# A causal mask added by VectorE in a PSUM bank in place of a matmul per score tile

## The chip, the core and the metric

The kernel runs on one core of a Trainium2 chip. The metric is the device time of one execution in microseconds. A core has TensorE (matmuls, called PE in the profile), VectorE (DVE), ScalarE (ACT), GpSimd (POOL) and SyncE (SP, here only DMAs), each with its own instruction stream. They meet only through semaphores that the kernel sets and waits on by hand.

## What is computed

One transformer layer on an input of 4 batches, 1024 tokens and 256 features. A layer norm feeds a latent attention with 16 heads and a linear layer with binarised weights, and both are added to the input. Cut to what matters:

```python
q = jnp.concatenate([queries_c, queries_r], axis=-1)      # 128 + 64 wide, 16 heads
k = jnp.concatenate([keys_c, keys_r], axis=-1)
scores = jnp.einsum('bhqd,bhkd->bhqk', q, k) * scale
causal = jnp.triu(jnp.ones((s, s), dtype=bool), k=1)
scores = jnp.where(causal[None, None], jnp.float32(-1000000000.0), scores)
probs = jax.nn.softmax(scores, axis=-1)
ctx = jnp.einsum('bhqk,bhkd->bhqd', probs, values)
...
x = x + attention(layernorm(x)) + linear(layernorm(x))
```

Only the 128 x 128 block on the diagonal of a tile of 128 queries needs a mask: keys to its right are never computed into the softmax, and keys to its left are all allowed.

## The kernel before

**Steps, blocks, items.** A step is one pair of heads of one batch: 8 pairs by 4 batches are 32 steps. A step has four blocks n = 0 to 3. A block joins a long and a short tile of 128 queries (7 and 0, 6 and 1, 5 and 2, 4 and 3), for both heads, which gives four score items x = 0 to 3 in the order long, short, long, short. An item is therefore as wide as its keys: 1024 and 128 in block 0, 896 and 256 in block 1, 768 and 384 in block 2, 640 and 512 in block 3. The code counts blocks through the whole run with g.

**The way of an item.** PE writes the scores, with their sign turned, into a slot of `ring`, a PSUM ring of only two slots of 1024 columns that items share with the projections for the next step (`ROPE_K`, `QUERY_X`, `QUERY_Y`, three a step). Each chunk of up to 512 keys takes three matmuls in a split precision (lines 1334 to 1336). VectorE reads the slot, subtracts a column, writes `probs` and takes the minimum along the row (`minimum`, line 1069). That frees the slot. ScalarE takes the exponential (`exponent`, 883). PE transposes the probabilities in groups of up to two key tiles for two heads, four transposes a group, into one of two `turn` banks (`turn_group`, 1359). ScalarE copies the high part of a group out (`turned_high`, 892), VectorE subtracts it for the low part (`turned_low`, 1079). Five groups make a block. PE then multiplies by the latent values (`weigh_group`, 1377 and 1378, into `u_ps`) and by the output weights (`output`, 1397 and 1398, into `o_ps`), with copies by ScalarE (897, 906) and VectorE (`u_low`, 1085), and VectorE adds the result to `acc` (`accumulate`, 1115, twice, the second waiting for the first).

**What sets the order.** Every engine's order is written by hand in a `sequence(g)` of its own, in order and without skipping. PE's transposes of block g - 1 lie between the scores of block g. Before `turn_group` writes a bank it waits until `turned_low` has read the group two before; before a group of a tile begins it waits for the exponentials of both heads.

**The mask.** `mask(g, x)` on PE waits for the ring slot (`slot_left`: until the entry two before has been read) and multiplies a bfloat16 identity by a bfloat16 tile `mask_bf`, which holds 1e30 above the diagonal and 0 elsewhere. The product begins the accumulation in the diagonal block, and the last chunk of the scores adds to it. `turn_group(g, i, (g', x), ...)` puts the masks that it is given ahead of its last transpose, sometimes two at once:

```python
                        if (t, h) == (tiles - 1, 1):
                            for block_g, x in masked:
                                mask(block_g, x)
```

So it is the mask that waits for the slot, and the scores that follow need no wait of their own for it.

Of the kernel before, what the change touches and what calls it, by code (L numbers as in the profile page):

```python
# [30 lines left out]
ALU = mybir.AluOpType  # L31
# [3 lines left out]
P = 128  # L35
# [60 lines left out]
def is_block(g):  # L96
    return 0 <= g < STEPS * BLOCKS
# [382 lines left out]
def layer(nc, T, x, wp_dram, wv_dram, out):  # L480


    with ExitStack() as ctx:
# [3 lines left out]
        def sem(name):  # L487
            return ctx.enter_context(nc.semaphore(name))

        ident, ident_bf, mask_bf = T["ident"], T["ident_bf"], T["mask_bf"]  # L490
# [54 lines left out]
        min_ready = sem("min_ready")  # L545
# [9 lines left out]
        def slot_of(entry):  # L555

            return ITEM[entry] % 2
# [457 lines left out]
        def _(dve):  # L1015
# [210 lines left out]
        def _(pe):  # L1226
# [84 lines left out]
            def mask(g, x):  # L1311

                if not is_block(g):
                    return
                qt, entry = LONG_SHORT[g % BLOCKS][x % 2], ("score", g, x)
                slot_left(entry)
                pe.matmul(ring[slot_of(entry)][:, KEY_COLUMN[qt] + qt * P:KEY_COLUMN[qt] + (qt + 1) * P], ident_bf[:, :], mask_bf[:, :],  # L1317
                          start=True, stop=False, skip_group_check=True)

            def scores(g, x, c):  # L1320

                if not is_block(g):
                    return
                h, w = divmod(x, 2)
                qt, slot, entry = LONG_SHORT[g % BLOCKS][w], g // BLOCKS % 2, ("score", g, x)
                queries = slice(qt * P, (qt + 1) * P)
                qh, ql = q_hi[slot][h][:, queries], q_lo[slot][h][:, queries]
                kh, kl = k_hi[slot][h], k_lo[slot][h]

                first_key, width = KEY_CHUNKS[qt][c]  # L1330
# [9 lines left out]
            def turn_group(g, i, *masked):  # L1340
# [12 lines left out]
                for t in range(tiles):  # L1353
                    for h in range(2):
                        kt = first_kt + t
                        if (t, h) == (tiles - 1, 1):
                            for block_g, x in masked:
                                mask(block_g, x)
                        mm = pe.transpose(turn[r % 2][:, (2 * t + h) * P:(2 * t + h + 1) * P],  # L1359
                                          probs_of(g, w, h)[:, kt * P:(kt + 1) * P], ident[:, :])  # L1360
# [52 lines left out]
            def sequence(g):  # L1413
# [3 lines left out]
                if n == 0:  # L1417
# [3 lines left out]
                    turn_group(g - 1, 1, (g, 0))  # L1421
# [5 lines left out]
                    turn_group(g - 1, 2, (g, 1))  # L1427
# [4 lines left out]
                    turn_group(g - 1, 3, (g, 2))  # L1432
# [9 lines left out]
                    turn_group(g, 0, (g, 3))  # L1442
                    weigh_group(g - 1, 3)
                    scores(g, 3, 0)
                    turn_group(g, 1, (g + 1, 0))
                elif n == 1:
# [4 lines left out]
                    turn_group(g - 1, 2, (g, 1))  # L1451
# [4 lines left out]
                    turn_group(g - 1, 3, (g, 2))  # L1456
# [4 lines left out]
                    turn_group(g - 1, 4, (g, 3))  # L1461
# [4 lines left out]
                    turn_group(g, 0, (g + 1, 0))  # L1466
                elif n == 2:
                    scores(g, 0, 0)
                    scores(g, 0, 1)
                    turn_group(g - 1, 1, (g, 1))  # L1470
                    weigh_group(g - 2, 4)
                    scores(g, 1, 0)
                    turn_group(g - 1, 2, (g, 2))
# [5 lines left out]
                    turn_group(g - 1, 3, (g, 3))  # L1479
# [10 lines left out]
                    turn_group(g, 0, (g + 1, 0), (g + 1, 1))  # L1490
                    output(g - 2, 1)
                else:
# [8 lines left out]
                    turn_group(g - 1, 2, (g, 2))  # L1501
# [9 lines left out]
                    turn_group(g - 1, 4, (g, 3))  # L1511
# [44 lines left out]
```

## Time and profile before

| | |
|---|---|
| median of 3 runs | 1517.84 us (1513.96 to 1517.99) |
| the profiled execution | 1516.44 us, of which 1514.4 us are the span |
| PE busy | 1435.9 us (95%) |
| ScalarE busy | 1219.0 us (80%) |
| VectorE busy | 1160.3 us (77%) |
| GpSimd busy | 946.8 us (63%) |
| mean granted TensorE clock | 0.987 |

The span runs from the first to the last instruction. Busy time is summed over a span whose first 156 us prepare weights, so that a share over the whole understates what an engine does in the steps. Steps that carry no work for the next batch take just under 40 us each. In each of the first three batches the last three steps also prepare the next batch and take longer.

### The profile page before, as it was taken

How to read it: one execution, taken by the hardware profiler on the slowest of the kernel's cores; microseconds unless marked ns; L12 is line 12 of the kernel's file. 1: busy time of each engine (PE TensorE's matmuls, PEld its weight loads, DVE VectorE, ACT ScalarE, POOL GpSimd, SP SyncE). 2: the span in 40 equal slices, each digit the busy share in tenths (PEclk: the TensorE clock that was granted, in tenths of full speed). 3: DMA queues.
4: the chain of work that ended last, by engine and by line, in shares of the span. 5: the costliest groups of instructions: out<-in, count | busy, mean ns of one | idle time of the engine just before them, and what ended most of it. 6: DMA issues, size and time to landing. Idle time of an engine off the chain costs nothing.

```text
span 1514.4 us, 27903 instructions
## 1 busy us (share of the span) xinstructions
PE 1435.9 (95%) x9878; PEld 1300.0 (86%) x9878; DVE 1160.3 (77%) x2768; ACT 1219.0 (80%) x2568; POOL 946.8 (63%) x476
## 2 busy tenths in 40 slices
PE   1976999999999999999999999999999999999998
PEld 1855899989889999989889899989889999999987
DVE  2444688888677888888767888888767788888887
ACT  0532888899868888899878888899878888888886
POOL 3010777776767677766867577776866577777750
PEclk9996999999999999999999999999999999999998
DMA  9445232222032432222023432211123422111110
GB/s 209 160 160 124 60 88 60 60 60 60 22 88 74 108 88 60 61 60 57 19 79 89 109 88 60 60 47 44 44 73 95 109 60 59 48 47 50 53 29 29
DMA packets 46819, 111.62 MB, mean 74 GB/s; under 512 B 13600, under 2 KB 22816, under 8 KB 46688
## 3 DMA queue, kind: packets, MB, share of 16 engines
q1 hardware_dynamic: 36912, 103.31, 24.9%
q10 hardware_dynamic: 8720, 3.70, 1.1%
q0 software_dynamic: 1056, 2.89, 0.7%
q8 instruction: 79, 1.29, 0.4%
q14 instruction: 52, 0.43, 0.1%
HBM read 50.10 MB, written 13.63 MB: 42 GB/s over the span
## 4 chain that ended last, share of the span: by engine, by line
PE 80%; ACT 6%; DVE 4%; SPq 1%; POOL 1%; issue 1%; DMA 1%; DVEq 0%; POOLq 0%; ACTq 0%
PE turn L1359 15%; PE ring L1304 10%; PE u_ps L1377 8%; PE u_ps L1378 8%; PE ring L1336 8%; PE ring L1334 8%; PE ring L1335 8%; PE o_ps L1397 4%; PE o_ps L1398 4%; ACT probs L883 2%; PE ring L1317 2%; PE ring L1266 2%; PE ring L1272 1%; DVE probs L1069 1%; ACT probs_hi L892 1%; DVE probs_lo L1079 1%
## 5 line engine op out<-in xcount | busy, mean ns | idle before, releaser
L1069 DVE TENSOR_SCALAR_CACHE_REDUCE probs<-ring,c_t 128x1024 f32<-128x1024 f32 (+7 forms) x512 | 413.7, 809 | 105.7 <-PE ring L1336 103.5
L1079 DVE TENSOR_TENSOR probs_lo<-turn,probs_hi 128x512 fp32r<-128x512 f32 (+1 forms) x640 | 400.9, 630 | 70.3 <-ACT probs_hi L892 65.8
L892 ACT ACTIVATE probs_hi<-turn 128x512 fp32r<-128x512 f32 (+1 forms) x640 | 351.0, 550 | 110.2 <-PE turn L1359 105.2
L883 ACT ACTIVATE probs<-probs,row_min 128x1024 f32<-128x1024 f32 (+7 forms) x512 | 394.4, 771 | 10.8 <-DVE probs L1069 8.3
L1359 PE MATMUL turn<-ident,probs 128*128 128x128 f32 x2304 | 385.8, 275 | 7.6 <-ACT probs L883 5.2
L1359 PEld LDWEIGHTS turn<-ident,probs 128*128 128x128 f32 x2304 | 286.4, 140 | 33.9 <-ACT probs L883 11.2
L1377 PE MATMUL u_ps<-probs_hi,kv_nat 128*128 128x256 f32 x1152 | 314.6, 302 | 0.3 <-DVE probs_lo L1079 0.3
L1378 PE MATMUL u_ps<-probs_lo,kv_nat 128*128 128x256 f32 x1152 | 289.9, 281 | 0.0
L1334 PE MATMUL ring<-k_hi,q_hi 128*128 128x512 f32 (+2 forms) x768 | 280.0, 365 | 0.0
L1336 PE MATMUL ring<-k_hi,q_lo 128*128 128x512 f32 (+2 forms) x768 | 264.3, 344 | 0.0
L1335 PE MATMUL ring<-k_lo,q_hi 128*128 128x512 f32 (+2 forms) x768 | 262.9, 342 | 0.0
L1115 DVE SCALAR_TENSOR_TENSOR acc<-o_ps,row_inv,acc 128x256 f32<-128x256 f32 x480 | 229.9, 479 | 36.2 <-PE o_ps L1398 31.4
L1377 PEld LDWEIGHTS u_ps<-probs_hi,kv_nat 128*128 128x128 f32 x1152 | 218.9, 190 | 1.3 <-DVE probs_lo L1079 0.5
L1378 PEld LDWEIGHTS u_ps<-probs_lo,kv_nat 128*128 128x128 f32 x1152 | 218.5, 190 | 0.0
L608 POOL TENSOR_TENSOR k_rope<-k_rope,cos 128x1024 f32<-128x1024 f32 x31 | 74.4, 2401 | 194.9 <-DMA swapped<-k_rope 194.8
L615 POOL TENSOR_TENSOR k_lo<-k_rope,k_hi 64x1024 fp32r<-64x1024 f32 x62 | 148.2, 2390 | 58.0 <-ACT k_hi L861 55.5
L1336 PEld LDWEIGHTS ring<-k_hi,q_lo 128*128 128x128 f32 x768 | 145.0, 189 | 13.6
L608 POOL TENSOR_TENSOR q_x<-q_x,cos 64x1024 f32<-64x1024 f32 x31 | 74.4, 2399 | 131.1 <-DMA swapped<-q_x 131.1
L1334 PEld LDWEIGHTS ring<-k_hi,q_hi 128*128 128x128 f32 x768 | 147.0, 191 | 7.2
L1335 PEld LDWEIGHTS ring<-k_lo,q_hi 128*128 128x128 f32 x768 | 145.7, 190 | 7.4
L608 POOL TENSOR_TENSOR swapped<-swapped,sin 128x1024 f32<-128x1024 f32 x62 | 148.7, 2399 | 4.9
L1397 PE MATMUL o_ps<-wv,u_hi 128*128 128x256 f32 x512 | 145.2, 305 | 4.2 <-DVE acc L1115 2.3
(176 smaller groups left out, 2631.5 us busy)
## 6 DMA issues: line engine op xcount, KB each, us to landing
wp<-wp_scratch SPq DMA_DIRECT2D x32, 640.0 KB, 4.2
wv<-wv_scratch SPq DMA_DIRECT2D x32, 512.0 KB, 3.3
swapped<-k_rope SPq DMA_DIRECT2D x128, 128.0 KB, 2.3
swapped<-q_y SPq DMA_DIRECT2D x64, 128.0 KB, 2.3
swapped<-q_x SPq DMA_DIRECT2D x64, 128.0 KB, 2.3
wp_scratch<-wp_parts SPq DMA_DIRECT2D x8, 640.0 KB, 3.4
wv_scratch<-wv_parts SPq DMA_DIRECT2D x8, 512.0 KB, 4.3
k_hi<-qb_kv_hi SPq DMA_DIRECT2D x16, 256.0 KB, 3.8
```

The source lines that it names most:

```text
L608: engine.tensor_tensor(to, a, b, op).then_inc(rope_step, 1)
L883: act.activation(p, p, ACT.Exp, scale=-1.0, bias=row_min[:, r:r + 1], accum_out=row_sum[:, g % 4, w, h:h + 1]).then_inc(exp_ready, 1)
L892: act.activation(probs_hi[:, r % 4, 0:width], turn[r % 2][:, 0:width], ACT.Identity).then_inc(turned_hi, 1)
L1069: dve.tensor_scalar(probs_of(g, w, h), ring[slot_of(entry)][:, KEY_COLUMN[qt]:KEY_COLUMN[qt] + keys], c_t[b % 2][:, qt, ds(pair * 2 + h, 1 ...
L1079: dve.tensor_tensor(probs_lo[:, r % 4, 0:width], turn[r % 2][:, 0:width], probs_hi[:, r % 4, 0:width].bitcast(F32), ALU.subtract).then_inc ...
L1115: dve.scalar_tensor_tensor(out=acc[:, qt, :], in0=o_ps[:, h, :], scalar=inv, in1=start[:, qt, :], op0=ALU.mult, op1=ALU.add).then_inc((acc ...
L1334: pe.matmul(to, qh, kh[:, keys], start=not masked, stop=False, skip_group_check=masked)
L1335: pe.matmul(to, qh, kl[:, keys], start=False, stop=False, skip_group_check=masked)
L1336: mm = pe.matmul(to, ql, kh[:, keys], start=False, stop=True, skip_group_check=masked)
L1359: mm = pe.transpose(turn[r % 2][:, (2 * t + h) * P:(2 * t + h + 1) * P], probs_of(g, w, h)[:, kt * P:(kt + 1) * P], ident[:, :])
L1377: pe.matmul(u_ps[:, 0:2 * P], kv_nat[:, kt, :], probs_hi[:, r % 4, cols], start=(kt == 0), stop=False)
L1378: mm = pe.matmul(u_ps[:, 0:2 * P], kv_nat[:, kt, :], probs_lo[:, r % 4, cols], start=False, stop=(kt == qt))
```

## The change

The mask matmuls go, 16 a step and 512 in all, with the function that made them. The scores' first chunk waits for the ring slot itself, and all chunks start a fresh accumulation. VectorE adds the same mask tile to the diagonal block of the slot, in PSUM and in place, and waits on a semaphore of its own, `mask_added`, before it takes the minimum. The weights, the ring, the order of everything else and the other engines are as before.

```diff
@@ minimum, VectorE
                 dve.wait_ge(ring_full, ITEM[entry] + 1)
+                diagonal = ring[slot_of(entry)][:, KEY_COLUMN[qt] + qt * P:KEY_COLUMN[qt] + keys]
+                dve.tensor_tensor(diagonal, diagonal, mask[:, :], ALU.add).then_inc(mask_added, 1)
+                dve.wait_ge(mask_added, g * SCORE_ITEMS + x + 1)
                 dve.tensor_scalar(probs_of(g, w, h), ring[slot_of(entry)][:, KEY_COLUMN[qt]:KEY_COLUMN[qt] + keys],
@@ scores, PE
-                masked = c == len(KEY_CHUNKS[qt]) - 1
-                pe.matmul(to, qh, kh[:, keys], start=not masked, stop=False, skip_group_check=masked)
-                pe.matmul(to, qh, kl[:, keys], start=False, stop=False, skip_group_check=masked)
-                mm = pe.matmul(to, ql, kh[:, keys], start=False, stop=True, skip_group_check=masked)
-                if masked:
+                if c == 0:
+                    slot_left(entry)
+                pe.matmul(to, qh, kh[:, keys], start=True, stop=False)
+                pe.matmul(to, qh, kl[:, keys], start=False, stop=False)
+                mm = pe.matmul(to, ql, kh[:, keys], start=False, stop=True)
+                if c == len(KEY_CHUNKS[qt]) - 1:
                     mm.then_inc(ring_full, 1)
@@ turn_group, PE
-                        if (t, h) == (tiles - 1, 1):
-                            for block_g, x in masked:
-                                mask(block_g, x)
@@ sequence, PE (15 calls lose their masks)
-                    turn_group(g - 1, 3, (g, 2))
+                    turn_group(g - 1, 3)
```

On PE, in block 0 of a step in the middle of the run, item 2's mask stood inside the group of transposes ahead of item 2's scores. The rows are one instruction each (or a run of equal ones), with the tile written, the tiles read and what it waits for. Before:

```order
 L1359 MATMUL turn<-ident,probs 128x128 [waits turned_ready,exp_ready]
 L1359 MATMUL turn<-ident,probs 128x128 x2
 L1317 MATMUL ring<-mask_bf,ident_bf 128x128 [waits min_ready]
 L1359 MATMUL turn<-ident,probs 128x128
 L1334 MATMUL ring<-k_hi,q_hi 128x512 [waits k_lo_ready,hi_step,rope_step]
```

The same place after the change:

```order
 L1349 MATMUL turn<-ident,probs 128x128 [waits turned_ready,exp_ready]
 L1349 MATMUL turn<-ident,probs 128x128 x3
 L1329 MATMUL ring<-k_hi,q_hi 128x512 [waits k_lo_ready,min_ready,hi_step,rope_step]
 L1330 MATMUL ring<-k_lo,q_hi 128x512
 L1331 MATMUL ring<-k_hi,q_lo 128x512
```

The wait for `min_ready`, which frees the slot, moved behind the last transpose, to the first matmul of the scores.

On VectorE, in blocks 2 and 3 of a step, each minimum (`probs,row_min<-ring,c_t`) stood alone. Before:

```order
 L1069 TENSOR_SCALAR probs,row_min<-ring,c_t 128x640 [waits ring_full]
 L1085 TENSOR_TENSOR u_pair<-u_ps,u_hi 64x256 [waits u_hi_ready]
 L1079 TENSOR_TENSOR probs_lo<-turn,probs_hi 128x512 [waits turned_hi]
 L1069 TENSOR_SCALAR probs,row_min<-ring,c_t 128x512 [waits ring_full]
 L1115 SCALAR_TENSOR_TENSOR acc<-o_ps,row_inv,acc 128x256 [waits o_full,inv_ready]
 L1079 TENSOR_TENSOR probs_lo<-turn,probs_hi 128x512 [waits turned_hi]
```

The same place, at the start of block 3, after the change:

```order
 L1070 TENSOR_TENSOR ring<-ring,mask_bf 128x128 [waits ring_full]
 L1072 TENSOR_SCALAR probs,row_min<-ring,c_t 128x640 [waits mask_added]
 L1088 TENSOR_TENSOR u_pair<-u_ps,u_hi 64x256 [waits u_hi_ready]
 L1082 TENSOR_TENSOR probs_lo<-turn,probs_hi 128x512 [waits turned_hi]
 L1070 TENSOR_TENSOR ring<-ring,mask_bf 128x128 [waits ring_full]
 L1072 TENSOR_SCALAR probs,row_min<-ring,c_t 128x512 [waits mask_added]
 L1118 SCALAR_TENSOR_TENSOR acc<-o_ps,row_inv,acc 128x256 [waits o_full,inv_ready]
 L1082 TENSOR_TENSOR probs_lo<-turn,probs_hi 128x512 [waits turned_hi]
```

Each minimum now has the addition directly ahead of it, and the wait for the scores moved to the addition. The minimum waits for the addition.

## Rows read from the trace of the kernel before

**Rows 1.** The page, busy time of each engine, share of the span, instructions

```profile
PE 1435.9 (95%) x9878; PEld 1300.0 (86%) x9878; DVE 1160.3 (77%) x2768; ACT 1219.0 (80%) x2568; POOL 946.8 (63%) x476
```

**Rows 2.** The page, the chain that ended last, by engine and by line

```profile
PE 80%; ACT 6%; DVE 4%; SPq 1%; POOL 1%; issue 1%; DMA 1%; DVEq 0%; POOLq 0%; ACTq 0%
PE turn L1359 15%; PE ring L1304 10%; PE u_ps L1377 8%; PE u_ps L1378 8%; PE ring L1336 8%; PE ring L1334 8%; PE ring L1335 8%; PE o_ps L1397 4%; PE o_ps L1398 4%; ACT probs L883 2%; PE ring L1317 2%; PE ring L1266 2%; PE ring L1272 1%; DVE probs L1069 1%; ACT probs_hi L892 1%; DVE probs_lo L1079 1%
```

**Rows 3.** Windows: one plain step, then two that also prepare a batch

```profile
core 0: us, PE busy (x) PEld busy (x) DVE busy (x) ACT busy (x) POOL busy (x), PEclk, DMA share, GB/s
...
540.42:580.30 39.88, 39.88 (x290) 36.95 (x289) 33.75 (x81) 35.48 (x76) 28.85 (x13) 1.00 0.29 84
...
400.30:447.00 46.70, 45.18 (x275) 38.01 (x275) 29.70 (x68) 33.29 (x65) 32.51 (x14) 1.00 0.22 60
447.00:500.10 53.10, 52.19 (x384) 48.45 (x383) 41.12 (x98) 43.23 (x93) 29.43 (x14) 1.00 0.36 90
```

**Rows 4.** Groups by line and shape on VectorE: count, busy us, mean ns

```profile
L1079 DVE TENSOR_TENSOR probs_lo<-turn,probs_hi 128x512 fp32r<-128x512 f32 x512 | 347.6, 683 | 69.8 <-ACT probs_hi L892 65.3
...
L1079 DVE TENSOR_TENSOR probs_lo<-turn,probs_hi 128x256 fp32r<-128x256 f32 x128 | 53.2, 416 | 0.5 <-ACT probs_hi L892 0.5
...
L1069 DVE TENSOR_SCALAR_CACHE_REDUCE probs<-ring,c_t 128x128 f32<-128x128 f32 x64 | 22.1, 346 | 36.9 <-PE ring L1336 36.9
```

**Rows 5.** Timeline of VectorE: start, us, instruction, [idle before, releaser]

```profile
576.43 1.28 DVE L1069 TENSOR_SCALAR_CACHE_REDUCE probs<-ring,c_t 128x1024 f32<-128x1024 f32 x1
...
589.08 0.48 DVE L1115 SCALAR_TENSOR_TENSOR acc<-o_ps,row_inv,acc 128x256 f32<-128x256 f32 x1 [1.11 <-PE o_ps L1398]
...
594.12 0.49 DVE L1069 TENSOR_SCALAR_CACHE_REDUCE probs<-ring,c_t 128x256 f32<-128x256 f32 x1 [0.30 <-PE ring L1336]
...
594.53 1.00 DVE L1115 SCALAR_TENSOR_TENSOR acc<-o_ps,row_inv,acc 128x256 f32<-128x256 f32 x2
...
596.79 1.01 DVE L1069 TENSOR_SCALAR_CACHE_REDUCE probs<-ring,c_t 128x768 f32<-128x768 f32 x1
...
598.10 0.60 DVE L1069 TENSOR_SCALAR_CACHE_REDUCE probs<-ring,c_t 128x384 f32<-128x384 f32 x1
598.63 1.28 DVE L1079 TENSOR_TENSOR probs_lo<-turn,probs_hi 128x512 fp32r<-128x512 f32 x2
...
603.16 0.69 DVE L1079 TENSOR_TENSOR probs_lo<-turn,probs_hi 128x512 fp32r<-128x512 f32 x1 [0.59 <-ACT probs_hi L892]
...
608.47 0.68 DVE L1079 TENSOR_TENSOR probs_lo<-turn,probs_hi 128x512 fp32r<-128x512 f32 x1
...
611.17 0.75 DVE L1069 TENSOR_SCALAR_CACHE_REDUCE probs<-ring,c_t 128x512 f32<-128x512 f32 x1 [0.16 <-PE ring L1336]
```

**Rows 6.** Timeline of PE, same columns

```profile
577.90 0.22 PE L1317 MATMUL ring<-mask_bf,ident_bf 128*128 128x128 bf16 x1
577.95 0.28 PE L1359 MATMUL turn<-ident,probs 128*128 128x128 f32 x1
577.99 0.48 PE L1334 MATMUL ring<-k_hi,q_hi 128*128 128x512 f32 x1
...
598.09 0.48 PE L1334 MATMUL ring<-k_hi,q_hi 128*128 128x512 f32 x1
...
599.69 0.27 PE L1359 MATMUL turn<-ident,probs 128*128 128x128 f32 x1
...
609.52 0.27 PE L1359 MATMUL turn<-ident,probs 128*128 128x128 f32 x1
```

**Rows 7.** Timeline of ScalarE, same columns

```profile
572.15 0.72 ACT L883 ACTIVATE probs<-probs,row_min 128x512 f32<-128x512 f32 x1
...
572.86 1.11 ACT L816 ACTIVATE k_rope<-ring,bias_p 128x1024 f32<-128x1024 f32 x1
...
575.20 0.59 ACT L892 ACTIVATE probs_hi<-turn 128x512 fp32r<-128x512 f32 x1
```

More of the change, by code:

```diff
@@ L488, in sem @@
             return ctx.enter_context(nc.semaphore(name))
-        ident, ident_bf, mask_bf = T["ident"], T["ident_bf"], T["mask_bf"]
+        ident, mask = T["ident"], T["mask_bf"]
         w_down, b_down, bias_p = T["w_down"], T["b_down"], T["bias_p"]
@@ L544, in layer @@
         swap_done, rope_step, hi_step, k_lo_ready = sem("swap_done"), sem("rope_step"), sem("hi_step"), sem("k_lo_ready")
-        min_ready = sem("min_ready")
+        mask_added, min_ready = sem("mask_added"), sem("min_ready")
         exp_ready = sem("exp_ready")
@@ L1309, in project @@
                     project_pair(g // BLOCKS + 1, k)
[L1311 to L1318, printed above, removed]
             def scores(g, x, c):
@@ L1332, in scores, with turn_group @@
                 to = ring[slot_of(entry)][:, KEY_COLUMN[qt]:][:, keys]
-                masked = c == len(KEY_CHUNKS[qt]) - 1
-                pe.matmul(to, qh, kh[:, keys], start=not masked, stop=False, skip_group_check=masked)
-                pe.matmul(to, qh, kl[:, keys], start=False, stop=False, skip_group_check=masked)
-                mm = pe.matmul(to, ql, kh[:, keys], start=False, stop=True, skip_group_check=masked)
-                if masked:
+                if c == 0:
[4 more added lines that the diff above has]
+                if c == len(KEY_CHUNKS[qt]) - 1:
                     mm.then_inc(ring_full, 1)
-            def turn_group(g, i, *masked):
+            def turn_group(g, i):
                 if not is_block(g):
-                    for block_g, x in masked:
-                        mask(block_g, x)
                     return
@@ L1355, in turn_group @@
                         kt = first_kt + t
-                        if (t, h) == (tiles - 1, 1):
-                            for block_g, x in masked:
-                                mask(block_g, x)
                         mm = pe.transpose(turn[r % 2][:, (2 * t + h) * P:(2 * t + h + 1) * P],
@@ L1420, in sequence @@
                     turn_group(g - 1, 0)
-                    turn_group(g - 1, 1, (g, 0))
+                    turn_group(g - 1, 1)
                     weigh_group(g - 2, 3)
@@ L1426, in sequence @@
                     scores(g, 0, 1)
-                    turn_group(g - 1, 2, (g, 1))
+                    turn_group(g - 1, 2)
                     output(g - 2, 0)
@@ L1441, in sequence @@
                     output(g - 2, 1)
-                    turn_group(g, 0, (g, 3))
+                    turn_group(g, 0)
                     weigh_group(g - 1, 3)
                     scores(g, 3, 0)
-                    turn_group(g, 1, (g + 1, 0))
+                    turn_group(g, 1)
                 elif n == 1:
@@ L1450, in sequence @@
                     output(g - 2, 0)
-                    turn_group(g - 1, 2, (g, 1))
+                    turn_group(g - 1, 2)
                     weigh_group(g - 2, 4)
@@ L1455, in sequence @@
                         begin("down", b + 1, 1)
-                    turn_group(g - 1, 3, (g, 2))
+                    turn_group(g - 1, 3)
                     scores(g, 2, 0)
@@ L1460, in sequence @@
                     weigh_group(g - 1, 1)
-                    turn_group(g - 1, 4, (g, 3))
+                    turn_group(g - 1, 4)
                     output(g - 2, 1)
@@ L1465, in sequence @@
                     weigh_group(g - 1, 3)
-                    turn_group(g, 0, (g + 1, 0))
+                    turn_group(g, 0)
                 elif n == 2:
@@ L1469, in sequence @@
                     scores(g, 0, 1)
-                    turn_group(g - 1, 1, (g, 1))
+                    turn_group(g - 1, 1)
                     weigh_group(g - 2, 4)
                     scores(g, 1, 0)
-                    turn_group(g - 1, 2, (g, 2))
+                    turn_group(g - 1, 2)
                     if pair == 6:
@@ L1478, in sequence @@
                     scores(g, 2, 1)
-                    turn_group(g - 1, 3, (g, 3))
+                    turn_group(g - 1, 3)
                     weigh_group(g - 1, 0)
@@ L1489, in sequence @@
                     weigh_group(g - 1, 3)
-                    turn_group(g, 0, (g + 1, 0), (g + 1, 1))
+                    turn_group(g, 0)
                     output(g - 2, 1)
@@ L1500, in sequence @@
                         begin("linear", b + 1, 1)
-                    turn_group(g - 1, 2, (g, 2))
+                    turn_group(g - 1, 2)
                     if pair == 7:
@@ L1510, in sequence @@
                     weigh_group(g - 1, 1)
-                    turn_group(g - 1, 4, (g, 3))
+                    turn_group(g - 1, 4)
                     weigh_group(g - 1, 2)
```

## The prediction

> **What bounds the kernel now.** I read the busy shares first. PE is busy for 95% of the span, ScalarE 80%, VectorE 77% [rows 1]. The chain that ended last says the same: 80% of it is PE's own work, VectorE has 4%, and the mask's line 1317 has 2% [rows 2]. The average hides how near VectorE is, because the span begins with a preparation in which it does little. So I read one plain step by itself. It takes 39.88 us, PE is busy for all of them at a granted clock of 1.00, and VectorE for 33.75 us [rows 3]. VectorE has 6.13 us left in a step, ScalarE 4.4. Then I read the timelines, to see where the 6.13 us lie. They lie in a few waits, among them 1.11 us ahead of an accumulation in block 1, 0.30 at 594.12 and 0.59 at 603.16 [rows 5]. The first two end with PE, the third with ScalarE. Between them VectorE runs through without a pause long enough to be marked, and between 575 and 576 it runs right behind ScalarE.
>
> **What PE gets back.** Matmuls overlap, so the 0.22 us of a mask's row aren't its price. The transpose behind it starts 0.05 us later [rows 6], and 2% of the chain, some 29 us over 512 masks, is 0.056 us each [rows 2]. 16 of them are 0.9 us of PE in a step, 29 us in the run. That is the most that the change can bring: the floor is 39.0 us a step.
>
> **What VectorE pays.** No row of before adds on VectorE with its output in PSUM, so I bound it. The subtraction `turned_low` has the same form of operation with one input in PSUM: 683 ns for 512 columns and 416 for 256 [rows 4]. That is 1.043 ns a column and a fixed part of 149 ns, so 128 columns come to 283 ns. Then comes the wait for its own result. The accumulations are such a pair: two of 0.48 us take 1.00 us [rows 5], which leaves 0.04 us between end and start. I take 0.28 + 0.04 = 0.32 us for an addition and call it d. The upper bound is the dearest 128-column row, the minimum with 346 ns [rows 4]: d = 0.39. The lower bound goes by instructions that don't wait for each other: two `turned_low` of 0.68 us take 1.28 us [rows 5], so the second starts 0.08 us before the first ends. If the minimum started behind the addition like that, d would be 0.28 - 0.08 = 0.20. I take 0.32, because the row with a wait on its own engine is the nearer one.
>
> The Trainium skill weighs in here. Its page "VectorE: DVE Perf Modes", section "The DRAIN you can't avoid", says that the next Vector instruction doesn't begin until the pipe is empty, and that a semaphore behind each operation costs nothing extra. The rows don't agree: with a wait in between there are 0.04 us of gap, without one 0.08 us of overlap. By that rule d would be 0.20 and the sum that of the first rival below; by the rows it is 0.32.
>
> In a step that is 16 x 0.32 = 5.1 us. VectorE's work rises to 33.75 + 5.1 = 38.9 us, against PE's floor of 39.0. On paper it fits. But the idle time would have to lie where the additions lie, and VectorE is in order: behind each addition stand its minimum, then the low parts that free the `turn` banks, then ScalarE's exponentials.
>
> **Following the lateness through a step.** I go from one wait to the next, with PE on its old times, and note how late VectorE is.
> - Block 1: the wait of 1.11 us at 589.08 for PE makes VectorE whole again [rows 5]. Three minima follow up to 594.12. They cost 0.96 and the 0.30 at 594.12 gives some back, as do idle moments under 0.1 us that no row marks: 0.6 late.
> - Block 2: the minimum of 768 keys starts at 596.79 and lasts 1.01 [rows 5], so its slot is free at 597.8 + 0.6 + 0.32 = 598.7. PE wants it at 598.09 [rows 6]. PE waits 0.6 us.
> - The 384-key minimum at 598.10 makes it 1.2 late. The first of the two low parts behind it would have ended at 599.3 [rows 5] and now ends at 600.5. The transposes at 599.69 need the bank that it frees [rows 6]: PE is 0.8 late.
> - The two other minima of block 2 make it 1.9. The wait for ScalarE at 603.16 was 0.59 [rows 5]: 1.3 late at block 3.
> - Block 3: two minima make 1.9. The low part at 608.47 ends at 609.15 + 1.9 = 611.05; PE wants its bank at 609.52 [rows 6]: 1.5 late. The third makes 2.2, the 0.16 at 611.17 [rows 5] gives some back, the fourth makes 2.4.
> - Then through ScalarE. One step earlier the same minimum is followed by the exponential at 572.15, the evacuation at 572.86 and a chain of work to the high part at 575.20 [rows 7]. VectorE's block-0 minimum stands at 576.43 behind its low part [rows 5]. I give this stretch 0.1 us of slack: 2.3 late.
> - That minimum ends at 577.71 before, now 2.3 + 0.32 later. PE's mask wanted the slot at 577.90 and its scores start at 577.99, where the wait now stands [rows 6]. That is 0.3 us of slack, so PE is 2.3 us late there.
>
> Counted in d this is ten additions less about 0.9 us of slack. From here to 598.09 PE sets the pace. It regains 7 masks x 0.056 = 0.4 us; the minimum of the second long item with its exponential behind it gives 0.1 back. A plain step grows by 2.3 - 0.4 + 0.1 = 2.0 us, or 10 d - 1.2. It takes 41.9 us, with VectorE busy for 38.6 to 38.9 of them. What is late next is again VectorE: the masks removed behind block 2 bring PE nothing.
>
> **The sum.** Nine steps prepare the next batch as well. In two of those stretches VectorE is idle for 17.0 of 46.7 us and for 12.0 of 53.1 [rows 3], because PE has work for the batch between the blocks. There most additions find room, and I take 0.9 us a step, a bit under half. 23 x 2.0 + 9 x 0.9 = 54 us. The profiled execution took 1516.4 us, 1.4 below the median of the runs: 1516.4 + 54 = 1570 us. The preparation ahead of the steps and the DMAs aren't touched.
>
> **The rivals.**
> - *The additions start their minima back to back* (d = 0.20). For it: VectorE overlaps neighbours by 0.08 us. Against it: the gap of 0.04 us in the one pair that waits on itself [rows 5]. A plain step grows by 0.8 us, a heavy one by 0.4: 22 us, so 1538 us. 14 in 100. (The rule of the Trainium skill cited above, page "VectorE: DVE Perf Modes", leads to this case as well.)
> - *The dear end and what I don't follow* (d = 0.39, or PSUM as output costs more, or lateness that runs once more round through ScalarE, which has 4.4 us left). 10 d - 1.2 = 2.7: 23 x 2.7 + 9 x 1.2 = 73 us, 1590 us; with 3.3 us in a plain step 1605. 22 in 100.
> - *Faster: the pace stays PE's* because VectorE's idle time of 6.1 us takes the additions up. The place that decides is the slot of the first long item in blocks 0 and 2, where a free slot now precedes PE by some 0.3 us [rows 5, 6]. 10 d - 1.2 turns negative at d = 0.12, and only near d = 0.03 would all of the 0.9 us come back. Then each step loses 0.9: 1516 - 29 = 1488 us. For it speaks only that 38.9 is under 39.0. 5 in 100.
> - *It cancels*: the 0.9 us of PE pay for a smaller delay than I follow, d around 0.12 or more slack in ScalarE's stretch. 1517 us. 5 in 100.
>
> **How the numbers follow.** 1570 us is the likeliest, 54 in 100, with a range of its own of 1555 to 1585 from half the way to either bound of d. The range of 8 in 10 takes in both bounds, 1538 and 1590, and part of the worse end: 1535 to 1603. About 0.3% is what a measurement of this kernel can tell from no change. Faster by more than that has 5 in 100, within it 5, slower 90.
>
> **What would show it.** The step: a plain window of 41 to 43 us in place of 39.88, with PE busy for 94 to 97% of it. The addition's row: 280 to 300 ns, and its minimum starting 0.04 us behind its end. VectorE busy near 1160 + 512 x 0.28 = 1305 us, and a chain that ended last in which VectorE has 30% or more. The waits: PE, which hardly waits for VectorE now, should wait for the minimum at the scores' first matmul (line 1329) and for `turned_low` at the transposes (1349), most in blocks 2 and 3 and at item 2 of block 0, little in block 1. I would be wrong if the addition's row is near 0.2 us or over 0.35, if VectorE keeps waits of over 4 us a step because PE's lateness moves them rather than fills them (then the step is longer), if the heavy steps grow as much as the plain ones (20 us more) or if PE's waits make the granted clock fall from 1.00.

## The result: 3.3% slower, and the profile after

The changed kernel takes 1566.53 us (median of 4 runs, 1565.37 to 1568.35) against 1517.22 us of the kernel before. The ratio is 1.0332, with a 95% interval of 1.0317 to 1.0346. The forecast was 1570 us, and 1535 to 1603 as the range. Each experiment below was measured beside the kernel before, whose medians lay between 1514.96 and 1517.26 us, and its ratio is to that.

The page of the changed kernel: first the busy time of each engine with its share of the span, then the chain that ended last, by engine and by line.

```profile
PE 1463.3 (94%) x9366; PEld 1279.3 (82%) x9366; DVE 1293.1 (83%) x3280; ACT 1224.5 (78%) x2568; POOL 946.4 (61%) x476
...
PE 39%; DVE 36%; ACT 7%; issue 5%; POOL 3%; DMA 2%; SPq 1%; DVEq 0%; POOLq 0%; ACTq 0%
DVE probs_lo L1082 12%; DVE probs L1072 11%; PE ring L1307 8%; PE turn L1349 7%; DVE acc L1118 6%; PE ring L1329 4%; DVE ring L1070 4%; PE u_ps L1367 4%; PE ring L1330 3%; PE ring L1331 3%; PE u_ps L1368 3%; DVE u_pair L1088 2%; POOL k_rope L608 2%; PE ring L1269 2%; PE o_ps L1387 2%
```

PE still has the greatest busy share, one point less than in [rows 1]. A reader who stops there would call the kernel bound by PE. The chain shows the turn: VectorE's share of it was 4% and is 36% [rows 2]. Most of it is not the addition (line 1070, 4%) but the work behind it, the low parts (1082), the minima (1072) and the accumulations (1118), which now carry the additions' lateness. PE's modelled busy time rose by 27 us although 512 matmuls are gone. Part of a wait counts as a busy PE, which [rows 1] can't tell.

Windows of one plain step each, from `QUERY_X`'s first matmul to that of the next step, in the columns of [rows 3]. Before, late in the run, then after, twice:

```profile
1309.24:1349.12 39.88, 39.88 (x290) 36.94 (x289) 33.72 (x81) 35.59 (x76) 29.18 (x13) 1.00 0.21 57
```

```profile
554.12:596.11 41.99, 41.10 (x274) 36.30 (x273) 37.85 (x97) 35.65 (x75) 27.14 (x13) 1.00 0.27 79
...
1347.26:1389.28 42.02, 41.16 (x274) 36.36 (x273) 37.86 (x97) 35.67 (x75) 29.12 (x13) 1.00 0.20 55
```

A plain step takes 42.0 us in place of 39.88. The granted clock is 1.00 in both, so PE is not slower; it waits. Call the nine steps that also prepare the next batch heavy. Read over all 31 distances from step to step (by ScalarE's evacuation of `q_x`), the 22 plain ones grew by 44.6 us together, 2.0 each (not all took 39.88 us: the two ahead of the heavy ones took 41.2 and 40.3, and grew by 1.7 and 1.8), and the nine heavy ones by 1.0 us together. In that 1.0 us one heavy step of before weighs: it took 45.93 us where the two like it took 44.4, and fell by 1.6. The span grew by 49.3 us, from 1514.4 to 1563.7. The stretch behind the last of these marks, the last step and the drain, took 82.3 us before and 86.9 after, and the one ahead of the first mark was 1.0 us shorter.

The addition and the minimum of 128 columns, by line and shape as in [rows 4]:

```profile
L1070 DVE TENSOR_TENSOR ring<-ring,mask_bf 128x128 f32<-128x128 f32 x512 | 147.2, 288 | 62.7 <-PE ring L1331 62.6
...
L1072 DVE TENSOR_SCALAR_CACHE_REDUCE probs<-ring,c_t 128x128 f32<-128x128 f32 x64 | 22.5, 351 | 2.3
```

The addition takes 288 ns, against 283 forecast from [rows 4]. From its start to the minimum's start the median over all 512 pairs is 0.324 us: 0.289 and a gap of 0.035. That is d.

The waits of PE between 164 and 1500 us, matmuls and weight loads apart (us in total, times, longest):

```profile
PE ring L1329 <- DVE probs L1072: 6.9, 27, 0.3
PE o_ps L1387 <- DVE acc L1118: 6.2, 22, 0.3
...
PE u_ps L1367 <- DVE probs_lo L1082: 3.3, 7, 0.9
```

```profile
PEld turn L1349 <- DVE probs_lo L1082: 32.1, 100, 0.4
PEld ring L1329 <- DVE probs L1072: 13.5, 28, 0.5
```

PE waits for all three things that VectorE gives it: the bank of transposes, the ring slot and, not foreseen, the output bank `o_ps` that an accumulation has to read first.

### The profile page after: what moved, and what is told of

It reads as the page before. It is cut to its first block, busy times and chain, and to the rows that moved or that the text cites. A ratio compares the mean times of both kernels' runs of the same rounds, so it can differ in the third digit from the quotient of the medians.

```text
span 1563.7 us, 27447 instructions
## 1 busy us (share of the span) xinstructions
PE 1463.3 (94%) x9366; PEld 1279.3 (82%) x9366; DVE 1293.1 (83%) x3280; ACT 1224.5 (78%) x2568; POOL 946.4 (61%) x476
## 4 chain that ended last, share of the span: by engine, by line
PE 39%; DVE 36%; ACT 7%; issue 5%; POOL 3%; DMA 2%; SPq 1%; DVEq 0%; POOLq 0%; ACTq 0%
DVE probs_lo L1082 12%; DVE probs L1072 11%; PE ring L1307 8%; PE turn L1349 7%; DVE acc L1118 6%; PE ring L1329 4%; DVE ring L1070 4%; PE u_ps L1367 4%; PE ring L1330 3%; PE ring L1331 3%; PE u_ps L1368 3%; DVE u_pair L1088 2%; POOL k_rope L608 2%; PE ring L1269 2%; PE o_ps L1387 2%
## 5 line engine op out<-in xcount | busy, mean ns | idle before, releaser
L892 ACT ACTIVATE probs_hi<-turn 128x512 fp32r<-128x512 f32 (+1 forms) x640 | 344.8, 548 | 117.0 <-PE turn L1349 109.9
L1082 DVE TENSOR_TENSOR probs_lo<-turn,probs_hi 128x512 fp32r<-128x512 f32 (+1 forms) x640 | 399.5, 628 | 44.4 <-ACT probs_hi L892 40.2
L1072 DVE TENSOR_SCALAR_CACHE_REDUCE probs<-ring,c_t 128x1024 f32<-128x1024 f32 (+7 forms) x512 | 418.6, 818 | 18.1
L1349 PE MATMUL turn<-ident,probs 128*128 128x128 f32 x2304 | 363.8, 277 | 13.2 <-ACT probs L883 4.7
L1367 PE MATMUL u_ps<-probs_hi,kv_nat 128*128 128x256 f32 x1152 | 322.4, 306 | 3.7 <-DVE probs_lo L1082 3.5
L1349 PEld LDWEIGHTS turn<-ident,probs 128*128 128x128 f32 x2304 | 265.4, 140 | 60.3 <-DVE probs_lo L1082 35.9
L1329 PE MATMUL ring<-k_hi,q_hi 128*128 128x512 f32 (+2 forms) x768 | 281.0, 366 | 13.1 <-DVE probs L1072 8.7
L1367 PEld LDWEIGHTS u_ps<-probs_hi,kv_nat 128*128 128x128 f32 x1152 | 217.2, 189 | 13.5 <-DVE probs_lo L1082 9.5
L1070 DVE TENSOR_TENSOR ring<-ring,mask_bf 128x128 f32<-128x128 f32 x512 | 147.2, 288 | 62.7 <-PE ring L1331 62.6
```

Source lines behind the costliest of these rows:

```text
L892: act.activation(probs_hi[:, r % 4, 0:width], turn[r % 2][:, 0:width], ACT.Identity).then_inc(turned_hi, 1)
L1082: dve.tensor_tensor(probs_lo[:, r % 4, 0:width], turn[r % 2][:, 0:width], probs_hi[:, r % 4, 0:width].bitcast(F32), ALU.subtract).then_inc ...
L1329: pe.matmul(to, qh, kh[:, keys], start=True, stop=False)
L1367: pe.matmul(u_ps[:, 0:2 * P], kv_nat[:, kt, :], probs_hi[:, r % 4, cols], start=(kt == 0), stop=False)
```

## Where a step loses its 2 us

Both kernels run the same 9366 matmuls in the same order once the masks are taken out, so each can be paired with itself. The difference of their starts, in the plain step of [rows 6] and relative to the scores of item 2 in block 0 (577.99 before, 593.98 after):

| place, start before | PE's lateness, us | forecast for the stretch |
|---|---|---|
| block 0, item 2's scores, 577.99 | 0 | |
| block 1, the second pair of low parts used, 594.38 | 0.28 | not seen |
| block 2, the last transpose ahead of item 2's scores, 598.05 | 0.25 | |
| block 2, item 2's scores, 598.09 | 0.74 | slot 0.6 late |
| block 2, transposes, 599.69 | 0.94 | 0.8 |
| block 3, first output, 603.23 | 1.34 | not seen |
| block 3, transposes, 609.52 | 1.58 | 1.5 |
| next block 0, item 2's scores, 617.87 | 2.45 | 2.3 |

The forecast's lateness was counted from VectorE's wait at 589.08 in block 1, where I had let it be 0, and with PE on its old times. On the table's base its figures are 0.3 lower, because PE was to be 0.3 us earlier at 598.05: 0.3, 0.5, 1.2 and 2.0. This step grew by 2.46 us in all, more than the one ahead of it (2.11). VectorE also takes statistics for the next batch in it; that they are the cause is not shown. In the plain step late in the run PE is 0.06 us earlier ahead of item 2's scores of block 2, and then 0.42, 0.61, 1.02 (the first output), 1.28 and 2.15 late. At most places where a mask is gone PE gains 0.05 to 0.06 us, and at the waits it loses more than that.

The timeline of VectorE and of PE in the changed kernel, at the slot of block 2's item 2 (start, us, engine, instruction, idle before and releaser):

```profile
612.83 0.67 DVE L1082 TENSOR_TENSOR probs_lo<-turn,probs_hi 128x512 fp32r<-128x512 f32 x1
613.42 0.28 DVE L1070 TENSOR_TENSOR ring<-ring,mask_bf 128x128 f32<-128x128 f32 x1
613.74 1.02 DVE L1072 TENSOR_SCALAR_CACHE_REDUCE probs<-ring,c_t 128x768 f32<-128x768 f32 x1
```

```profile
613.96 0.60 PE L1349 MATMUL turn<-ident,probs 128*128 128x128 f32 x4
614.82 0.50 PE L1329 MATMUL ring<-k_hi,q_hi 128*128 128x512 f32 x1 [0.26 <-DVE probs L1072]
```

The low part ends at 613.50 and the addition starts 0.08 us before that. The minimum starts 0.04 behind the addition's end and ends at 614.76, and the scores into its slot start 0.06 later. Before, the slot was free at 597.80 and PE came at 598.09 [rows 5, 6].

## The experiments

Where a step is named, it is the plain one late in the run, as above. The windows that are quoted stand in the columns of [rows 3].

**1. No mask at all.** The changed kernel without its addition; the causal mask is left out of the result. PE's wait for the ring slot stays in its new place.

```diff
-                diagonal = ring[slot_of(entry)][:, KEY_COLUMN[qt] + qt * P:KEY_COLUMN[qt] + keys]
-                dve.tensor_tensor(diagonal, diagonal, mask[:, :], ALU.add).then_inc(mask_added, 1)
-                dve.wait_ge(mask_added, g * SCORE_ITEMS + x + 1)
```

> Leaves the causal mask out: neither the matmul nor the addition. It measures what PE gets back alone. Theory (the masks' 0.056 us each lie on PE's path, and VectorE's additions then lose more): 0.9 us less in a plain step than before (39.0 in place of 39.9), 1487 to 1492 us. Rival (the mask matmuls fill moments in which PE would wait anyway, so that there was nothing to gain): 1513 to 1518 us, as before.

Measured: 1491.92 us, ratio to before 0.9835 (0.9816 to 0.9853). The window:

```profile
1290.30:1329.50 39.20, 39.20 (x275) 36.15 (x273) 33.47 (x81) 35.40 (x76) 29.14 (x13) 1.00 0.21 59
```

The gain on PE is real: 24.5 us, and 0.68 us in a step, where 0.9 were forecast. The 0.68 is 0.042 us a mask and not 0.056. Each matmul of before can be paired with itself in this run, and the starts show where the difference goes. In this step PE gains 0.05 to 0.06 us at 15 of the 16 places, as forecast, and loses 0.22 us again at one, in block 3, where it now reaches a low part before VectorE is done with it:

```profile
1325.32 0.69 DVE L1079 TENSOR_TENSOR probs_lo<-turn,probs_hi 128x512 fp32r<-128x512 f32 x1
```

```profile
1326.07 0.38 PE L1364 MATMUL u_ps<-probs_hi,kv_nat 128*128 128x256 f32 x1
```

The low part ends at 1326.01. In the kernel before the same low part ended at 1345.49 and PE used it at 1345.73. So PE meets VectorE's pace in one place of the step even without additions.

Of the 23.2 us by which the span shrank, 13.1 lie in the nine heavy steps, 1.5 each, and 8.0 in the 22 plain ones (one of them grew by 1.6). A heavy step gains more than 16 masks of 0.056 are worth, because the wait for the slot is late in this run too (see runs 7 and 12). The additions thus cost 2.8 us a plain step (39.20 to 42.02), of which PE's saving pays 0.7, and 1.6 us a heavy one.

**2. Additions without a wait behind them.** The result goes to a spare tile and the minimum reads the slot unmasked, so the mask is left out.

```diff
-                dve.tensor_tensor(diagonal, diagonal, mask[:, :], ALU.add).then_inc(mask_added, 1)
-                dve.wait_ge(mask_added, g * SCORE_ITEMS + x + 1)
+                if g + x > 0:
+                    dve.wait_ge(mask_added, g * SCORE_ITEMS + x)
+                dve.tensor_tensor(scratch[:, :], diagonal, mask[:, :], ALU.add).then_inc(mask_added, 1)
```

The wait that is left is for the addition of the item before, long done.

> The addition writes to a spare SBUF tile instead of the ring, so the minimum behind it has no wait for it (the mask is left out of the result). Same number of instructions, same operation. Theory (an addition costs its 0.29 us, 0.04 of gap and the overlap of 0.08 that its neighbour loses, and about ten of them lie on the chain of a step): each is 0.12 us cheaper, a plain step 1.1 us shorter than in the changed kernel (41.0 in place of 42.1), 1536 to 1542 us. Rival (a wait between two VectorE instructions costs nothing, the Trainium skill's rule): within 4 us of the changed kernel, 1563 to 1570.

Measured: 1522.63 us, ratio 1.0042 (1.0028 to 1.0056). The addition's group and the window:

```profile
L1073 DVE TENSOR_TENSOR scratch<-ring,mask_bf 128x128 f32<-128x128 f32 x512 | 142.2, 278 | 72.2 <-PE ring L1333 71.6
```

```profile
1314.01:1354.24 40.23, 40.20 (x274) 36.20 (x273) 36.33 (x97) 35.73 (x76) 28.22 (x13) 1.00 0.21 57
```

The minimum now starts 0.082 us before the addition's row ends, and 0.198 us behind its start. That is 0.126 us less than 0.324 each time, and 44 us less in the run. About 0.01 of the 0.126 is the shorter row (278 against 288 ns, with its output outside PSUM); the rest is the wait on the engine's own result.

The rule of the Trainium skill (page "VectorE: DVE Perf Modes", section "The DRAIN you can't avoid"), that a semaphore behind each operation costs nothing extra, doesn't hold here. The same section does say that a next operation which isn't held starts earlier, and the overlap of 0.08 us in the rows without a wait agrees with that.

The step is 1.79 us shorter, which is 14 times 0.126 and not ten times: nearly all additions of a step lie on the chain. The time is lower than I expected for that reason.

**3. Each addition twice.**

```diff
-                dve.wait_ge(mask_added, g * SCORE_ITEMS + x + 1)
+                dve.wait_ge(mask_added, 2 * (g * SCORE_ITEMS + x) + 1)
+                dve.tensor_tensor(diagonal, diagonal, mask[:, :], ALU.add).then_inc(mask_added, 1)
+                dve.wait_ge(mask_added, 2 * (g * SCORE_ITEMS + x) + 2)
```

> Every addition is made twice, each with its wait. Theory A (about ten additions of a step lie on the chain and the others in VectorE's waits): 10 x 0.32 = 3.2 us more in a plain step, 1645 to 1660 us. Theory B (VectorE has become the bound by its load alone, so every addition counts): 16 x 0.32 = 5.2 us more, 1700 to 1735 us. With the waits that the changed kernel still has in a step (about 4 us) I expect something between, nearer A.

Measured: 1692.29 us, ratio 1.1159 (1.1140 to 1.1179); a step of 46.33 us, 4.31 more. The second addition starts 0.335 us before the minimum, so the step grew by 13 times that. The time lies between the two theories, nearer B than I had written. The busy time in the window shows why theory B doesn't hold in full:

```profile
1452.37:1498.70 46.33, 42.02 (x275) 36.30 (x273) 42.63 (x113) 36.33 (x75) 29.02 (x13) 1.00 0.18 50
```

VectorE still idles for 3.7 us of 46.33, as for 4.2 of 42.02 before the doubling. Waits stay with double the load.

**4. Additions one instruction earlier.** In blocks 2 and 3 another instruction stands between addition and minimum; one of the seven places:

```diff
-                    turned_low(g - 1, 1)
-                    minimum(g, 1)
+                    add_mask(g, 1)
+                    turned_low(g - 1, 1)
+                    minimum(g, 1, True)
```

> In blocks 2 and 3 seven of eight additions stand one VectorE instruction earlier, so that this instruction covers the wait for the addition; the last one and those of blocks 0 and 1 stay. Theory (0.12 us of each addition is its wait and the lost overlap): seven on the chain save 0.8 us in a plain step, 1545 to 1552 us. Rival (what counts is how late the low part ahead of the minimum is, and that is now behind an addition of 0.29 us; or the scores are not there yet one instruction earlier): 1566 us or more.

Measured: 1557.25 us, ratio 1.0269 (1.0251 to 1.0287): 9 us faster than the changed kernel, half of what was expected. A step takes 41.64 us, 0.38 less, where 7 x 0.12 = 0.84 were to be had. What VectorE waits for, 164 to 1500 us, in the changed kernel and then in this one:

```profile
DVE ring L1070 <- PE ring L1331: 54.1, 72, 4.1
```

```profile
DVE ring L1072 <- PE ring L1357: 61.6, 100, 4.1
```

28 more waits for scores that are not there one instruction earlier take back 7.5 us, 0.2 a step. The rest I didn't trace. The theory had a part of it, and so had the rival's second half; whether the later low parts count as well is not shown.

**5 and 6. Half of the blocks each.** The kernel before, with the mask of a set of items moved to VectorE; the others keep their matmul in its old place.

```diff
+ADDED = [(2, 0), (2, 1), (2, 2), (2, 3), (3, 0), (3, 1), (3, 2), (3, 3)]
...
+                if (n, x) in ADDED:
+                    diagonal = ring[slot_of(entry)][:, KEY_COLUMN[qt] + qt * P:KEY_COLUMN[qt] + keys]
+                    dve.tensor_tensor(diagonal, diagonal, mask_bf[:, :], ALU.add).then_inc(mask_added, 1)
+                    dve.wait_ge(mask_added, g // BLOCKS * len(ADDED) + ADDED.index((n, x)) + 1)
...
-                if not is_block(g):
+                if not is_block(g) or (g % BLOCKS, x) in ADDED:
...
+                if c == 0 and added:
+                    slot_left(entry)
```

> VectorE adds the mask in blocks 2 and 3 alone (8 items a step, on the stretch in which it ran without a pause); blocks 0 and 1 keep the mask matmul as before the change. Theory of place (an addition costs where lateness runs on to PE, and PE's waits in block 1 wipe out the rest): most of the loss, a plain step 1.2 to 1.6 us over the 39.9 of before, 1545 to 1555 us. Theory of load (VectorE's total work decides): half of it, or nothing, since 33.75 + 2.6 us stay well under 39: 1510 to 1525 us.

Measured: 1547.24 us, ratio 1.0202 (1.0186 to 1.0218), a step of 41.37 us.

> The complement: additions in blocks 0 and 1 alone. Theory of place: their lateness ends at the waits of blocks 0 and 1 but for the three ahead of block 2; PE gets 8 x 0.056 = 0.45 us back, the step stays within 0.3 us of 39.9: 1508 to 1525 us. Theory of load: the same as the other half.

Measured: 1526.73 us, ratio 1.0067 (1.0052 to 1.0083), a step of 40.25 us.

Eight additions cost 1.5 us a step in one half and 0.4 in the other, though VectorE gets the same work. Place decides, not load. But the half of blocks 0 and 1 is not as nearly free as I had thought: it came out 2 us over the upper end.

**7. The mask matmuls directly ahead of their scores.** No addition; the masks stay on PE, and the slot's wait moves as in the change.

```diff
                 if c == 0:
+                    mask(g, x)
...
-                        if (t, h) == (tiles - 1, 1):
-                            for block_g, x in masked:
-                                mask(block_g, x)
...
```

> No addition: all mask matmuls stay on PE, but each stands directly ahead of its scores, which moves the wait for the ring slot as the change does (one transpose later, up to ten matmuls for the short item of block 0). It measures the moved wait alone. Theory (PE waits some 7 us in all at the masks of before, in the steps with batch work): 0 to 6 us less, 1510 to 1517 us. Rival (the mask costs more between scores than between transposes): slower.

Measured: 1530.75 us, ratio 1.0092 (1.0076 to 1.0107): the rival. PE's timeline of this kernel, then of the kernel before, at the same place:

```profile
629.38 0.28 PE L1380 MATMUL u_ps<-probs_lo,kv_nat 128*128 128x256 f32 x1
629.50 0.23 PE L1318 MATMUL ring<-mask_bf,ident_bf 128*128 128x128 bf16 x1
629.54 0.37 PE L1341 MATMUL ring<-k_hi,q_hi 128*128 128x256 f32 x1
629.74 0.28 PE L1342 MATMUL ring<-k_lo,q_hi 128*128 128x256 f32 x1
```

```profile
629.01 0.22 PE L1317 MATMUL ring<-mask_bf,ident_bf 128*128 128x128 bf16 x1
629.07 0.28 PE L1359 MATMUL turn<-ident,probs 128*128 128x128 f32 x1
629.10 0.36 PE L1377 MATMUL u_ps<-probs_hi,kv_nat 128*128 128x256 f32 x1
629.31 0.28 PE L1378 MATMUL u_ps<-probs_lo,kv_nat 128*128 128x256 f32 x1
```

Matmuls of 256 columns follow each other by 0.12 us. One behind a mask or a transpose starts 0.03 to 0.04 us after it and takes 0.20 until the next one starts. For a transpose that is no extra price: transposes follow each other by 0.109 us, and 0.03 + 0.20 is as long as 0.109 + 0.12. A mask of its own between two such matmuls costs 0.04 + 0.20 + 0.12 in place of 0.12 + 0.12, which is 0.12 us, against 0.056 among transposes. In a step it comes to 0.8 us (39.88 to 40.68). The late wait pays some of that back in the heavy steps: paired with the kernel before, PE gains 0.83 us at one place of such a step. So this run says nothing clean on the moved wait, and run 12 was made for that.

**8. Three additions in free places.** As in 5, with `ADDED = [(0, 1), (0, 3), (1, 0)]`.

> Only three additions a step, where VectorE waits for PE soon after: the short items of block 0 (x = 1 and 3) and the first of block 1, with a wait of 1.11 us behind it. The 13 other masks stay on PE in their places. Theory of place: VectorE's 1.0 us of work cost nothing and PE gets 3 x 0.056 us back: 5 us less than before, about 1511 us. Rival (any addition on VectorE or its exponential on ScalarE is late for someone): same as before or slower, 1516 to 1525 us.

Measured: 1510.78 us, ratio 0.9965 (0.9953 to 0.9977), a step of 39.73 us, 0.15 less than before.

**9 and 10. Five and six.** As in 5, with `(2, 2)` and `(2, 3)` as well, and with `(1, 1)` on top.

> The three additions of the last such kernel and two more, for items 2 and 3 of block 2, which stand ahead of VectorE's wait of 0.59 us for ScalarE. Theory of place: two additions of 0.32 us just fill that wait, PE gets 5 x 0.056 us back in a step: a plain step of 39.6 us, about 1507 us (1504 to 1510). Rival (item 2's later end is felt by the exponential and the transposes behind it): 1511 to 1518 us.

> The five and one more, for item 1 of block 1, whose lateness of 0.32 us meets a slack of 0.30 before block 2. Theory: 6 x 0.056 us back, 1504 to 1509 us; as the slacks are used up it may be no better than the five.

Measured: 1511.92 us, ratio 0.9980 (0.9969 to 0.9992), and 1511.90 us, ratio 0.9975 (0.9965 to 0.9985). Run 9 came out in its rival's range and run 10 no better: the further additions bring nothing over three. The step of run 9 takes 39.81 us. Its rows show where it loses, and it is not where the rival had it:

```profile
1325.96 0.48 DVE L1120 SCALAR_TENSOR_TENSOR acc<-o_ps,row_inv,acc 128x256 f32<-128x256 f32 x1
```

```profile
1326.59 0.35 PE L1405 MATMUL o_ps<-wv,u_hi 128*128 128x256 f32 x1
```

The accumulation of block 2, behind both additions, reads the output bank until 1326.44, and PE's first output of block 3 into it starts 0.15 us later. In the kernel before 0.66 us lay between the two. This one place costs 0.22 us, and the five masks that are gone bring 0.28. VectorE's wait of 0.59 us would have taken the additions up, but the accumulation that PE waits for stands ahead of it. The transposes behind item 2 are not late.

**11. Three additions in bad places.** As in 5, with `ADDED = [(3, 0), (3, 1), (3, 2)]`.

> Also three additions a step, but for items 0 to 2 of block 3, where VectorE runs without a pause and the low parts behind them are what PE waits for. Theory of place: some 0.4 us late at the scores of block 0 and 0.17 us regained, a plain step of 40.1 to 40.2 us, 1521 to 1526 us. Theory of load (VectorE's total work decides, the same as with the three in free places): 1511 us.

Measured: 1524.67 us, ratio 1.0060 (1.0045 to 1.0076), a step of 40.41 us. The windows of run 8 and of this one:

```profile
1305.32:1345.05 39.73, 39.73 (x288) 36.86 (x287) 34.66 (x84) 35.47 (x76) 29.21 (x13) 1.00 0.21 57
```

```profile
1314.77:1355.18 40.41, 40.13 (x287) 36.80 (x286) 34.36 (x84) 35.68 (x76) 29.75 (x13) 1.00 0.21 56
```

The place where run 11 loses most, 0.43 us, in block 3:

```profile
1344.42 0.33 PE L1367 MATMUL turn<-ident,probs 128*128 128x128 f32 x1 [0.28 <-DVE probs_lo L1084]
```

The same three additions and the same three matmuls fewer, and VectorE busy for 34.7 and 34.4 us: 0.15 us less than before in one, 0.53 more in the other.

**12. The moved wait alone.** The changed kernel, with PE waiting for the slot where the mask matmuls stood. The edit is shown against the kernel before.

```diff
             def mask(g, x):
                 qt, entry = LONG_SHORT[g % BLOCKS][x % 2], ("score", g, x)
                 slot_left(entry)
-                pe.matmul(ring[slot_of(entry)][:, ...], ident_bf[:, :], mask_bf[:, :], start=True, ...)
```

> The changed kernel with its additions, but PE waits for the ring slot where the mask matmuls stood: ahead of a group's last transpose (for the short item of block 0 some ten matmuls earlier, for both items of block 3 at the end of block 2). It isolates the moved wait. Theory (VectorE is late at the slot of the first long item in blocks 0, 2 and 3, so a later wait lets one transpose of 0.12 us go ahead): the step loses 0.1 to 0.4 us, 1569 to 1580 us. Rival (VectorE's own chain sets the pace and the wait's place on PE does not matter): 1564 to 1568 us.

Measured: 1580.66 us, ratio 1.0429 (1.0411 to 1.0446), 14 us slower than the changed kernel and just over the theory's range. But the plain step takes 42.05 us, the same as with the late wait, so the theory's 0.1 to 0.4 us a step isn't there: where PE waits for the slot makes no difference to a plain step. The loss lies in the heavy steps, 12.5 us over the nine, for example 53.8 us in place of 52.6 and 46.2 in place of 44.4. The waits of PE for a minimum, 164 to 1500 us, in this run and in the changed kernel:

```profile
PE turn L1360 <- DVE probs L1072: 18.7, 32, 1.6
```

```profile
PE ring L1329 <- DVE probs L1072: 6.9, 27, 0.3
```

The longest waits, of 1.6 and 1.5 us, stand in two of the three kinds of heavy step, at a last transpose whose slot is not free. With the late wait PE does that transpose, and work for the next batch behind it, first. There the moved wait helps the change.

## Why the prediction was right

**What bounds the kernel, and d.** Right. The addition took 288 ns and 0.324 us to the minimum's start (forecast 0.283 and 0.32). Run 2 shows what the own wait costs, 0.126 us with 0.01 for the other output, as the rows of before had it (0.12). The first rival, that an addition lets its minimum start at once, falls.

**What PE gets back.** Right in kind and mis-sized: 0.68 us a step (run 1), not 0.9. A mask is worth the 0.056 us that was read in its place, but PE gives 0.22 us of the sum back at a low part that VectorE has not finished.

**A plain step grows by 2.0 us.** Right: 42.0 from 39.88. The stations were right too: the slot in block 2, then the transposes of blocks 2 and 3, then the slot in block 0.

The formula 10 d - 1.2 has two errors, and that they cancelled at d = 0.32 is luck. More additions count: 14 (run 2) or 13 (run 3) for ten. The working itself lists twelve (three, four, four and one); I had counted the wait of 0.59 us at 603.16 as two additions fewer, but it is a fixed time and belongs to the slack, so that by the working's own stations the growth is 12 d - 1.8. And there is still more slack: with 13.5 d, the middle of the two counts, the step is 37.6 us + 13.5 d, so that 13.5 x 0.324 less 2.3 us against 39.88 gives 2.1. This formula is fitted to the three runs: it gives 40.3 us for run 2, where it took 40.23, and 46.5 for run 3, where 46.33. Mine would have given 40.7 and 45.3.

The step of the working that failed is the regaining between 577.99 and 598.09, "it regains 7 masks x 0.056 = 0.4 us". PE does gain 0.05 to 0.06 us at each of these masks. But it was 0.25 us later there in the step of the table, and only 0.06 earlier in the late plain step, not 0.3 earlier. It loses the gain at the slot of block 1's first item (0.13) and at the low parts of block 1 (0.2 late in the run, 0.5 around 594.38). The additions of block 1 reach PE inside block 1, and I had let VectorE's wait at 589.08 end all lateness. The wait for `o_ps`, which takes 0.52 us at the first output of block 3, was not in the working either.

**The heavy steps.** Mis-sized: 0.9 us each forecast, 0.1 measured. It is not that all additions find room there. They cost 1.6 us a heavy step (the changed kernel against run 1), and the masks that are gone and the late wait together pay 1.5 of it. With the wait in its old place a heavy step grows by 1.5 us (run 12).

**The sum.** In the profiled executions: 44.6 us in 22 plain steps for 44 forecast, 1.0 in the heavy ones for 8.1, and 4.6 in the last step with its drain for 2.0. The stretch ahead of the steps was 1.0 us shorter, where nothing was forecast. Together that is 49.3 us in place of 54.

**The moved wait.** I counted it as slack of 0.1 us in one place, in the plain step, where it brings nothing. It is worth 14 us in the run, nearly all in the heavy steps (run 12), and the sum had nothing for that. Without it the time would have been 1581 us, in the range still but 11 us over the forecast.

**The faster rival** put the turn at d = 0.12. As an estimate by 37.6 + 13.5 d, the change breaks even at d = 0.17, and the step of 39.20 us of run 1 would be reached at 0.12. No run has a d under 0.198, and run 2, which has it, was still 0.4% slower than before. What brought a gain was not a cheaper addition but fewer of them in the right places: run 8, three of 16, is 0.35% faster than the kernel before, and no run but the one without any mask was better.

**The signs.** The addition's row, the gap, the plain window, VectorE's share of the chain, PE's waits at lines 1329 and 1349 and a clock that stays at 1.00 came as named. Four did not. PE is busy for 98% of the window and not 94 to 97, since part of its waits counts as busy. VectorE's busy time rose to 1293 us and not 1305, and to 37.9 us in a step and not 38.6 to 38.9. PE's waits were to be few in block 1, and 0.5 us was lost there in the step of the table. And VectorE keeps 4.2 us of waits in a step, just over the 4 that I had named as a sign of being wrong: lateness is in part moved and not filled, as run 3 shows with 3.7 us of waits left under double the additions.

## What to carry to other kernels

VectorE, busy for 85% of a step, had no room for 13% more, although the sum stays under 100: here work fitted only where the engine waits for something that is itself not late, and those places are read one by one from a timeline. Before moving an operation from a saturated engine to a half idle one, follow the lateness of one such operation to the next wait that swallows it, and move only the operations that meet one soon. Count a dependent pair on VectorE with its wait and the overlap that it loses (0.12 us here), which for a tile of 128 columns is over a third of the price. When a wait moves with the change, price it by itself, in every kind of step.

## What was not expected of the hardware

- Where a small matmul stands can double its price. A mask of 128 columns took 0.056 us among transposes and 0.12 between two matmuls of 256 columns (the median starts of before and of run 7). Over a step, 16 of them cost 0.68 us among transposes and 1.48 ahead of the scores (runs 1 and 7).
- A waiting PE can read as a busy one: in run 2 its modelled busy time was 40.20 us of a step of 40.23, with the same matmuls that filled 39.20 in run 1. The idle time on PE's row is therefore no measure of how long it waits; the starts of paired matmuls are.
